# GpSimd's 512-column elementwise passes of a four-layer graph network, each made as two of 256 columns

## The chip, the cores and the metric

One core of one Trainium2 chip. The metric is the device time of the kernel in microseconds (us). The engines are TensorE (PE in the profile; PEld is its weight load), VectorE (DVE), ScalarE (ACT), GpSimd (POOL) and SyncE (SP).

## The reference, cut to what matters

128 graphs of 128 nodes with 256 features pass through four layers that share one adjacency matrix. Each layer takes `h = relu(layernorm(x))` and adds its result to `x`:

```python
h = relu(layernorm(x)); x = x + L0(h, adj)  # 4-head graph attention, elu, second attention, elu, ffn, layernorm
h = relu(layernorm(x)); x = x + L1(h, adj)  # 8-head attention: (softmax(q k^T) v) Wo^T + bo; its mask is adj == 0
h = relu(layernorm(x)); x = x + L2(h, adj)  # deg * (h Wi^T + b) + adj @ (h Wj^T)
h = relu(layernorm(x)); x = x + L3(h, adj)  # graph attention over 128 features, joined with them
```

Inside L0 the step `y = relu(out @ w1 + b1) @ w2 + b2 + out` is followed by a layernorm with `ln_gamma` and `ln_beta`.

## The kernel before, in words

The graphs are worked on in 64 pairs. The features of a pair lie in a slot of `xs` (128 partitions, 2 graphs of 256 columns; eight slots in rotation). Letters name stages: A and B are the heads of L0 and its first output, C is its second attention and ffn, D and F are L1, E is L2 and then L3.

Every engine runs the same loop, `rounds`: in round i it makes each step of its own list (`PE_ORDER`, `ACT_ORDER`, `DVE_ORDER`, `POOL_ORDER`) once, for pair i minus the number behind the step's name. So seven or more pairs are in work at a time, at different stages, and each engine's order is fixed by hand. A step waits at its head for semaphores of the steps before it (`done`, `both`, `before`) and counts up one of its own at its end.

Products are made from fp32 values split into a high part (rounded, type fp32r) and a low part (the rest), in three matmuls each. The split of a tile is an ACT copy to the high part and a subtraction for the low part.

GpSimd's list is `A_fleft A_fright A_rstd E_right E_rstd3 C_hb C_low B_lowh.1 D_xb E_fcopy E_rstd C_xb C_fcopy C_rstd E_xb D_rstd B_lowh.0`. Its steps are:

- `B_lowh` (line 464), once a graph: the low part of the upper 512 columns of `B_e`, for the matmuls `B_wh2` and `B_wh3` of PE (line 1191). The lower 512 columns are split by DVE (`B_lowl`, line 897).
- `C_low` (line 470): the low part of the ffn's hidden tile, 512 columns, for PE's `C_ffn` (line 1084, `pC<-w_high,C_hid_high`).
- `C_xb` (477), `D_xb` (487), `E_xb` (493): a bias row is added in place to the pair's slot, both graphs at once by `on_pair`, a broadcast. DVE's `C_x1` (945), `F_x2` (1002) and `E_mi` (1015) add to the slot later.
- `C_hb` (482): `C_h_t` plus `b2` into `C_hb_t`, for DVE's `C_y` (930).
- `E_fcopy` (lines 432 to 438): four small passes that split the two logit vectors of L3 in three bf16 parts. It waits for ACT's `E_hc` (699), and PE's `E_fT` (line 1200, `pE<-ident_bf,E_f`) waits for it.
- the `rstd` steps (413 and 415), which DVE's normalisations `A_z`, `D_z`, `E_z` and `E_z3` (all line 828) wait for, and others of up to 256 columns.

On DVE, `A_norm.0` and `A_norm.1` (line 881) scale the softmax of a graph, 512 columns, from SBUF to SBUF.

Of the kernel before, what the change touches and what calls it, by code (L numbers as in the profile page):

```python
# [4 lines left out]
ALU = mybir.AluOpType  # L5
ACT = mybir.ActivationFunctionType
AX = mybir.AxisListType
F32 = mybir.dt.float32
# [59 lines left out]
def gnn_stack(nc, x, adj, w_heads, a_heads, w_out, a_out, w1, b1, w2, b2, gamma, beta,  # L68
# [5 lines left out]
    K = D // P  # L74
    G = 2
    W = G * P
    H0 = w_heads.shape[0]
    HD = H0 * D
# [7 lines left out]
    with ExitStack() as ctx:  # L86
        def sb(name, shape, dt=F32):
            return ctx.enter_context(nc.sbuf_tensor(name, shape, dt))
# [4 lines left out]
        def sem(name):  # L93
            return ctx.enter_context(nc.semaphore(name))
# [19 lines left out]
        b2_b = sb("b2_b", [P, D])  # L114
        gamma_b = sb("gamma_b", [P, D])
        beta_b = sb("beta_b", [P, D])
# [3 lines left out]
        bo_b = sb("bo_b", [P, D])  # L120
        bl2_b = sb("bl2_b", [P, D])
        w3_w = sb("w3_w", [P, K, F3 + 2])

        def high_low(name, shape):
            return sb(name + "_high", shape, F32R), sb(name + "_low", shape, F32R)
# [30 lines left out]
        B_e = sb("B_e", [P, HD])  # L156
        B_hl_t = high_low("B_h", [P, HD])
# [5 lines left out]
        C_e, C_h_t = sb("C_e", [P, G, D]), sb("C_h_t", [P, G, D])  # L163
        C_hb_t = C_e
        C_hT_hl = high_low("C_hT", [P, K * W])
        C_hid_t = sb("C_hid_t", [P, K * W])
        C_hid_hl = high_low("C_hid", [P, K * W])
# [50 lines left out]
        S = {name: sem(name) for name in STEP_SEMAPHORES}  # L218
# [14 lines left out]
        def slot(g):  # L233
            return xs[:, (g // G) % PAIR_SLOTS, g % G, :]

        def pair_slot(p):
            return xs[:, p % PAIR_SLOTS, :, :]

        def done(eng, name, n):

            eng.wait_ge(S[name], n + 1)

        def both(eng, name, p):

            eng.wait_ge(S[name], G * p + G)
# [25 lines left out]
        def of_graph(make):  # L271

            return [lambda p, s=s: make(G * p + s, p, s) for s in range(G)]
# [7 lines left out]
        def on_pair(row):  # L281
            return row.unsqueeze(1).to_broadcast([P, G, D])
# [19 lines left out]
        def at_first(p, eng, signal, count):  # L302

            if p == 0:
                eng.wait_ge(signal, count)
# [49 lines left out]
        def _(pool):  # L355
# [104 lines left out]
            def B_lowh(g, p, s):  # L460

                done(pool, "B_highh", g)
                cols = slice(HD // 2, HD)
                pool.tensor_tensor(B_hl_t[1][:, cols], B_e[:, cols], B_hl_t[0][:, cols].bitcast(F32), ALU.subtract)\  # L464
                    .then_inc(S["B_lowh"], 1)

            def C_low(p):

                done(pool, "C_high", p)
                pool.tensor_tensor(C_hid_hl[1][:, :], C_hid_t[:, :], C_hid_hl[0][:, :].bitcast(F32), ALU.subtract)\  # L470
                    .then_inc(S["C_low"], 1)

            def C_xb(p):

                both(pool, "A_z", p)
                at_first(p, pool, weights_loaded, LOADED)
                pool.tensor_tensor(pair_slot(p), pair_slot(p), on_pair(beta_b[:, :]), ALU.add).then_inc(S["C_xb"], 1)

            def C_hb(p):

                both(pool, "C_h", p)
                pool.tensor_tensor(C_hb_t[:, :, :], C_h_t[:, :, :], on_pair(b2_b[:, :]), ALU.add).then_inc(S["C_hb"], 1)

            def D_xb(p):

                both(pool, "D_z", p)
                pool.tensor_tensor(pair_slot(p), pair_slot(p), on_pair(bo_b[:, :]), ALU.add).then_inc(S["D_xb"], 1)

            def E_xb(p):

                both(pool, "E_z", p)
                at_first(p, pool, dots_made, BIASES + 2)
                pool.tensor_tensor(pair_slot(p), pair_slot(p), on_pair(bl2_b[:, :]), ALU.add).then_inc(S["E_xb"], 1)

            def E_right(p):

# [3 lines left out]
                pool.tensor_tensor(right, right, E_h_t[:, :, 0:F3], ALU.add).then_inc(S["E_right"], 1)  # L500

            B_lowh = of_graph(B_lowh)
            rounds(pool, POOL_ORDER, {
                "A_rstd": rstd("A", "", A_mv, A_ve, A_rs), "C_rstd": rstd("C", "", C_mv, C_ve, C_rs),
# [3 lines left out]
                "C_fcopy": split_in_three("C", wh2[:, :, D:D + 2], C_f3, C_frest_t),  # L508
                "E_fcopy": split_in_three("E", E_h_t[:, :, F3:F3 + 2], E_f3, E_frest_t),
                "B_lowh.0": B_lowh[0], "B_lowh.1": B_lowh[1], "C_low": C_low,  # L510
                "C_xb": C_xb, "C_hb": C_hb, "D_xb": D_xb, "E_xb": E_xb, "E_right": E_right,
            }, {("A_fleft", 0): wh_low, ("B_lowh.0", 0): wout_low, ("C_hb", 0): other_low((W1, W2)),
                ("D_rstd", 0): other_low((WK, WV, WQ)), ("D_xb", 0): other_low((WO, WIJ))})
# [958 lines left out]
```

## Time and profile before

| | |
|---|---|
| runs | 2681.39, 2682.44, 2683.78 us; median 2682.44 |
| the profiled execution | 2683.62 us; its span, first to last instruction, 2681.8 us |
| PE, PEld busy | 2580.8 us (96%), 2333.0 us (87%) |
| DVE, ACT, POOL busy | 2304.7 (86%), 2061.2 (77%), 1248.4 us (47%) |
| granted TensorE clock, mean | 0.987 |
| DMA | 17 GB/s mean |

A busy share counts the time in which an engine has an instruction in work. PE's matmuls are pipelined, so one that is listed at 0.28 us can be followed by the next after 0.12 us. The idle time before an instruction, with what ended it, stands in square brackets in the timeline.

### The profile page before, as it was taken

What the parts mean: (1) busy time and instruction counts of PE and PEld (TensorE: products, weight loads), DVE (VectorE), ACT (ScalarE), POOL (GpSimd) and SP (SyncE); (2) the same over time, 40 slices, a digit from 0 to 9 for tenths busy, and PEclk for the clock granted to TensorE, in tenths of its full rate; (3) what the DMA queues carried; (4) which work ended last, traced back from release to release, by engine and by line L of the source; (5) the groups of instructions that cost most, each with busy time, mean ns of one, the idle gap of its engine ahead of it and who ended that gap; (6) DMA issues with size and microseconds to landing.
All of it is one profiled execution on the core that took longest, in us unless ns stands there. A gap on an engine that the chain in (4) does not pass through costs nothing.

```text
span 2681.8 us, 64380 instructions
## 1 busy us (share of the span) xinstructions
PE 2580.8 (96%) x21761; PEld 2333.0 (87%) x21761; DVE 2304.7 (86%) x8352; ACT 2061.2 (77%) x5708; POOL 1248.4 (47%) x2015
## 2 busy tenths in 40 slices
PE   4899999999999999999999999999999999999985
PEld 3789999998998998999999999899999899999874
DVE  5689889889888888888888888888988988988884
ACT  4688788787787887877877877878878878878752
POOL 3545445444444444454454454454544544544431
PEclk9999999999999999999999999999999999999986
DMA  4000000000000000000000000000000000000000
GB/s 131 1 2 9 17 17 9 17 17 14 13 17 13 13 17 17 10 17 17 10 17 17 10 17 17 10 17 17 9 17 17 9 17 17 10 17 13 9 9 12
DMA packets 41286, 44.29 MB, mean 17 GB/s; under 512 B 2816, under 2 KB 40448, under 8 KB 40832
## 3 DMA queue, kind: packets, MB, share of 16 engines
q1 hardware_dynamic: 40816, 39.14, 4.6%
q8 instruction: 175, 2.87, 0.5%
q14 instruction: 151, 1.24, 0.2%
q10 hardware_dynamic: 144, 1.05, 0.1%
HBM read 23.40 MB, written 16.78 MB: 15 GB/s over the span
## 4 chain that ended last, share of the span: by engine, by line
PE 70%; ACT 20%; POOL 4%; issue 3%; DVE 2%; SPq 1%; DMA 0%; ACTq 0%; DVEq 0%; POOLq 0%
PE pA L1084 12%; PE pB L1191 11%; PE pE L1084 7%; PE pB L1158 7%; PE pB L1084 7%; ACT probs L579 7%; PE pF L1315 4%; PE pC L1084 3%; ACT pA L573 3%; ACT B_h_high L613 2%; PE pF L1328 2%; PE pA L1302 2%; PE pC L1237 2%; ACT C_hid_t L649 2%; ACT whs L560 1%
## 5 line engine op out<-in xcount | busy, mean ns | idle before, releaser
L677 ACT ACTIVATE F_s_t<-F_s_t,F_m 128x128 f32<-128x128 f32 x1024 | 325.3, 395 | 0.9 <-DVE F_m L863 0.8
L1191 PE MATMUL pB<-wout_high,B_h_high 128*128 128x258 f32 x1024 | 307.4, 300 | 1.1 <-DVE B_h_low L897 1.1
L1191 PE MATMUL pB<-wout_low,B_h_high 128*128 128x258 f32 x1024 | 289.6, 283 | 0.0
L1191 PE MATMUL pB<-wout_high,B_h_low 128*128 128x258 f32 x1024 | 288.8, 282 | 0.0
L1158 PE MATMUL pB<-probs,whs 128*128 128x128 f32 x2048 | 285.4, 282 | 1.4 <-ACT wh L620 1.1
L1158 PEld LDWEIGHTS pB<-probs,whs 128*128 128x128 f32 x2048 | 254.2, 192 | 20.8 <-issue 2.4
L1084 PE MATMUL pA<-wh_high,A_hT_high 128*128 128x512 f32 x512 | 229.0, 447 | 9.5 <-POOL wh_low L388 8.4
L889 DVE SCALAR_TENSOR_TENSOR B_e<-B_e,pB 128x512 f32<-128x512 f32 x256 | 172.9, 675 | 71.7 <-ACT B_e L605 71.4
L464 POOL TENSOR_TENSOR B_h_low<-B_e,B_h_high 128x512 fp32r<-128x512 f32 x128 | 165.8, 1295 | 111.8 <-ACT B_h_high L613 111.8
L1084 PE MATMUL pA<-wh_high,A_hT_low 128*128 128x512 f32 x512 | 202.9, 396 | 0.0
L1084 PE MATMUL pA<-wh_low,A_hT_high 128*128 128x512 f32 x512 | 202.7, 396 | 0.0
L1191 PEld LDWEIGHTS pB<-wout_high,B_h_high 128*128 128x128 f32 x1024 | 193.9, 189 | 9.2 <-DVE B_h_low L897 1.9
L579 ACT ACTIVATE probs<-probs,A_m 128x128 f32<-128x128 f32 x512 | 198.2, 405 | 0.0
L1191 PEld LDWEIGHTS pB<-wout_low,B_h_high 128*128 128x128 f32 x1024 | 194.8, 190 | 2.7
L413 POOL TENSOR_TENSOR D_ve<-D_mv,eps 128x2 f32<-128x2 f32 x64 | 12.5, 195 | 395.2 <-DVE D_mv L821 395.2
L1191 PEld LDWEIGHTS pB<-wout_high,B_h_low 128*128 128x128 f32 x1024 | 193.8, 189 | 0.0
L470 POOL TENSOR_TENSOR C_hid_low<-C_hid_t,C_hid_high 128x512 fp32r<-128x512 f32 x64 | 83.2, 1300 | 236.1 <-ACT C_hid_high L546 236.1
L828 DVE TENSOR_SCALAR E_z_t<-xs,E_mv,E_rs 128x256 f32<-128x256 f32 x256 | 182.1, 731 | 3.2 <-POOL E_rs L415 3.2
L413 POOL TENSOR_TENSOR E_ve<-E_mv,eps 128x2 f32<-128x2 f32 x128 | 25.0, 195 | 333.8 <-DVE E_mv L821 333.8
L975 DVE TENSOR_REDUCE F_sum<-F_s_t 128x4 f32<-128x512 f32 x256 | 167.6, 676 | 0.2 <-ACT F_s_t L677 0.2
L613 ACT ACTIVATE B_h_high<-B_e 128x512 fp32r<-128x512 f32 x256 | 155.5, 640 | 7.6 <-DVE B_e L889 1.5
L605 ACT ACTIVATE B_e<-B_e 128x512 f32<-128x512 f32 x256 | 160.4, 627 | 0.1
(261 smaller groups left out, 10046.6 us busy)
## 6 DMA issues: line engine op xcount, KB each, us to landing
xs<-in_x SPq DMA_DIRECT2D x64, 256.0 KB, 2.7
out_x<-xs SPq DMA_DIRECT2D x64, 256.0 KB, 2.1
probs<-in_a_heads ACTq DMA_DIRECT2D x1, 1024.0 KB, 4.9
F_pT<-in_w_heads SPq DMA_DIRECT2D x2, 512.0 KB, 6.9
xs<-in_w_out SPq DMA_DIRECT2D x1, 1024.0 KB, 9.6
F_s_t<-in_wijT SPq DMA_DIRECT2D x1, 512.0 KB, 6.4
C_h_t<-in_a_out SPq DMA_DIRECT2D x1, 256.0 KB, 9.9
D_q_t<-in_w SPq DMA_DIRECT2D x1, 256.0 KB, 7.2
```

Of the source, the lines that this page charges most:

```text
L464: pool.tensor_tensor(B_hl_t[1][:, cols], B_e[:, cols], B_hl_t[0][:, cols].bitcast(F32), ALU.subtract)\
L579: last = act.activation(A_l[:, s, h, :], A_l[:, s, h, :], ACT.Exp, scale=-1.0, bias=A_m[:, s, h:h + 1], accum_out=A_sum[:, s, h:h + 1])
L605: act.activation(B_e[:, cols], B_e[:, cols], ACT.Exp, scale=-1.0).then_inc(S["B_exp" + part], 1)
L613: act.activation(B_hl_t[0][:, cols], B_e[:, cols], ACT.Copy).then_inc(S["B_high" + part], 1)
L677: last = act.activation(F_s_t[:, s, h, :], F_s_t[:, s, h, :], ACT.Exp, scale=-1.0, bias=F_m[:, s, h:h + 1])
L828: dve.tensor_scalar(z[:, s, :], slot(g), mv[:, s, 0:1], rs[:, s:s + 1], ALU.subtract, ALU.mult)\
L889: dve.scalar_tensor_tensor(out=e, in0=e, scalar=-1.0, in1=pB[:, bank, :], op0=ALU.add, op1=ALU.max)\
L975: dve.tensor_reduce(total, e, AX.X, ALU.add).then_inc(S["F_sum" + part], 1)
L1084: last = pe.matmul(dst, a, b, start=(i == 0), stop=(i == len(terms) - 1))
L1158: last = pe.matmul(pB[:, bank, (k % 4) * P:(k % 4 + 1) * P], whs[:, s, h, c * P:(c + 1) * P], attnT[:, s, h, :], start=True, stop=True)
L1191: last = pe.matmul(pB[:, 0, 0:D + 2], a, w[:, k, :], start=(k == 0 and i == 0), stop=(k == KH - 1 and i == 2))
L1315: last = pe.transpose(pF[:, c, j * P:(j + 1) * P], F_s_t[:, s, c * HPC + j, :], ident[:, :])
```

## The change

Each of the six steps makes its pass in two halves of 256 columns, one behind the other, with the semaphore counted up by the second. `B_lowh` runs twice a pair, so seven passes a pair become fourteen, and 448 passes in all become 896. The operands, the order of the steps, all waits and the other engines' programs stay as they are.

```diff
             def B_lowh(g, p, s):
 
                 done(pool, "B_highh", g)
-                cols = slice(HD // 2, HD)
-                pool.tensor_tensor(B_hl_t[1][:, cols], B_e[:, cols], B_hl_t[0][:, cols].bitcast(F32), ALU.subtract)\
-                    .then_inc(S["B_lowh"], 1)
+                for part in range(2):
+                    cols = slice(HD // 2 + part * HD // 4, HD // 2 + (part + 1) * HD // 4)
+                    last = pool.tensor_tensor(B_hl_t[1][:, cols], B_e[:, cols], B_hl_t[0][:, cols].bitcast(F32), ALU.subtract)
+                last.then_inc(S["B_lowh"], 1)
...
             def D_xb(p):
 
                 both(pool, "D_z", p)
-                pool.tensor_tensor(pair_slot(p), pair_slot(p), on_pair(bo_b[:, :]), ALU.add).then_inc(S["D_xb"], 1)
+                for s in range(G):
+                    last = pool.tensor_tensor(slot(G * p + s), slot(G * p + s), bo_b[:, :], ALU.add)
+                last.then_inc(S["D_xb"], 1)
...
```

`C_low` is cut in the same way as `B_lowh` (columns `c * W` to `(c + 1) * W` for c of 0 and 1), and `C_xb`, `C_hb` and `E_xb` in the same way as `D_xb`.

## Rows read from the trace of the kernel before

**Rows 1.** The page, part 1: busy time and share of each engine.

```profile
PE 2580.8 (96%) x21761; PEld 2333.0 (87%) x21761; DVE 2304.7 (86%) x8352; ACT 2061.2 (77%) x5708; POOL 1248.4 (47%) x2015
```

**Rows 2.** Busy time by stretch; columns PE, PEld, DVE, ACT, POOL busy, clock, DMA, GB/s.

```profile
1000.00:1500.00 500.00, 497.12 (x4257) 452.28 (x4256) 445.75 (x1636) 400.81 (x1125) 239.91 (x390) 1.00 0.05 14
```

**Rows 3.** The waits: who waited for whom, us in total, times, longest.

```profile
PE pE L1200 <- POOL E_f L438: 16.3, 61, 1.6
```

**Rows 4.** Timeline of PE in one round: start us, us, engine, line.

```profile
1324.57 0.60 PE L1151 MATMUL pA<-ident,probs 128*128 128x128 f32 x4
1325.40 0.22 PE L1200 MATMUL pE<-ident_bf,E_f 128*12 128x128 bf16 x1 [0.23 <-POOL E_f L438]
```

**Rows 5.** Timeline of POOL in the same round, and the same step a round on.

```profile
1312.92 1.28 POOL L482 TENSOR_TENSOR C_e<-C_h_t,b_b 128x512 f32<-128x512 f32 x1
...
1319.86 1.29 POOL L464 TENSOR_TENSOR B_h_low<-B_e,B_h_high 128x512 fp32r<-128x512 f32 x1 [0.74 <-ACT B_h_high L613]
1321.11 1.28 POOL L487 TENSOR_TENSOR xs<-xs,bo_b 128x512 f32<-128x512 f32 x1
1323.71 0.25 POOL L432 TENSOR_TENSOR E_f<-E_h_t,zeros 128x4 bf16<-128x4 f32 x1 [1.31 <-ACT E_h_t L699]
...
1324.32 0.63 POOL L436 TENSOR_TENSOR E_f<-E_frest_t,zeros 128x4 bf16<-128x4 f32 x1
1325.03 0.31 POOL L438 TENSOR_TENSOR E_f<-E_frest_t,E_f 128x4 bf16<-128x4 f32 x1
...
1326.46 1.27 POOL L477 TENSOR_TENSOR xs<-xs,beta_b 128x512 f32<-128x512 f32 x1
```

**Rows 6.** Timeline of DVE in the same round.

```profile
1313.49 1.20 DVE L828 TENSOR_SCALAR E_z_t<-xs,E_mv,E_rs 128x256 f32<-128x256 f32 x2
...
1321.90 0.69 DVE L930 TENSOR_TENSOR C_y_t<-pC,C_e 128x512 f32<-128x512 f32 x1
1322.51 0.40 DVE L828 TENSOR_SCALAR A_z_t<-xs,A_mv,A_rs 128x256 f32<-128x256 f32 x1
...
1324.21 0.68 DVE L881 TENSOR_TENSOR probs<-probs,A_rec 128x512 f32<-128x512 f32 x1
...
1326.53 1.35 DVE L828 TENSOR_SCALAR E_z_t<-xs,E_mv,E_rs 128x256 f32<-128x256 f32 x1
```

**Rows 7.** Timeline of ACT in the same round: what `E_fcopy` waits for.

```profile
1323.26 0.37 ACT L699 ACTIVATE E_h_t<-pE 128x260 f32<-128x260 f32 x1
```

**Rows 8.** Groups of POOL by line and shape: busy us, mean ns, idle before, releaser.

```profile
L487 POOL TENSOR_TENSOR xs<-xs,bo_b 128x512 f32<-128x512 f32 x64 | 82.8, 1294 | 0.0
L500 POOL TENSOR_TENSOR xs<-xs,E_h_t 128x256 f32<-128x256 f32 x64 | 43.8, 684 | 0.0
L413 POOL TENSOR_TENSOR D_ve<-D_mv,eps 128x2 f32<-128x2 f32 x64 | 12.5, 195 | 395.2 <-DVE D_mv L821 395.2
```

**Rows 9.** Who waited for line 464, and (second row) for line 470: us, times.

```profile
  PEld pB L1191: 0.2, 1
...
  PEld pC L1084: 0.2, 1
```

**Rows 10.** Groups of DVE by line and shape, columns as in rows 8.

```profile
L828 DVE TENSOR_SCALAR E_z_t<-xs,E_mv,E_rs 128x256 f32<-128x256 f32 x256 | 182.1, 731 | 3.2 <-POOL E_rs L415 3.2
L828 DVE TENSOR_SCALAR A_z_t<-xs,A_mv,A_rs 128x256 f32<-128x256 f32 x128 | 50.9, 398 | 1.2 <-POOL A_rs L415 1.2
```

**Rows 11.** The chain that ended last, in the drain: start us, us, what.

```profile
2567.33 1.11 DVE xs L945
...
2598.54 1.10 DVE xs L945
```

**Rows 12.** Timeline of POOL and DVE (last row: an undisturbed `C_x1`) beside that chain.

```profile
2566.89 1.26 POOL L493 TENSOR_TENSOR xs<-xs,bl_b 128x512 f32<-128x512 f32 x1 [1.09 <-DVE E_z_t L828]
...
2598.10 1.27 POOL L493 TENSOR_TENSOR xs<-xs,bl_b 128x512 f32<-128x512 f32 x1 [1.93 <-DVE E_z_t L828]
...
1336.56 0.48 DVE L945 SCALAR_TENSOR_TENSOR xs<-C_y_t,C_rs,xs 128x256 f32<-128x256 f32 x1
```

More of the change, by code:

```diff
@@ L462, in B_lowh @@
                 done(pool, "B_highh", g)
-                cols = slice(HD // 2, HD)
-                pool.tensor_tensor(B_hl_t[1][:, cols], B_e[:, cols], B_hl_t[0][:, cols].bitcast(F32), ALU.subtract)\
-                    .then_inc(S["B_lowh"], 1)
+                for part in range(2):
+                    cols = slice(HD // 2 + part * HD // 4, HD // 2 + (part + 1) * HD // 4)
+                    last = pool.tensor_tensor(B_hl_t[1][:, cols], B_e[:, cols], B_hl_t[0][:, cols].bitcast(F32), ALU.subtract)
+                last.then_inc(S["B_lowh"], 1)
             def C_low(p):
                 done(pool, "C_high", p)
-                pool.tensor_tensor(C_hid_hl[1][:, :], C_hid_t[:, :], C_hid_hl[0][:, :].bitcast(F32), ALU.subtract)\
-                    .then_inc(S["C_low"], 1)
+                for c in range(K):
+                    cols = slice(c * W, (c + 1) * W)
+                    last = pool.tensor_tensor(C_hid_hl[1][:, cols], C_hid_t[:, cols], C_hid_hl[0][:, cols].bitcast(F32),
+                                              ALU.subtract)
+                last.then_inc(S["C_low"], 1)
             def C_xb(p):
@@ L476, in C_xb @@
                 at_first(p, pool, weights_loaded, LOADED)
-                pool.tensor_tensor(pair_slot(p), pair_slot(p), on_pair(beta_b[:, :]), ALU.add).then_inc(S["C_xb"], 1)
+                for s in range(G):
+                    last = pool.tensor_tensor(slot(G * p + s), slot(G * p + s), beta_b[:, :], ALU.add)
+                last.then_inc(S["C_xb"], 1)
             def C_hb(p):
                 both(pool, "C_h", p)
-                pool.tensor_tensor(C_hb_t[:, :, :], C_h_t[:, :, :], on_pair(b2_b[:, :]), ALU.add).then_inc(S["C_hb"], 1)
+                for s in range(G):
+                    last = pool.tensor_tensor(C_hb_t[:, s, :], C_h_t[:, s, :], b2_b[:, :], ALU.add)
+                last.then_inc(S["C_hb"], 1)
             def D_xb(p):
                 both(pool, "D_z", p)
-                pool.tensor_tensor(pair_slot(p), pair_slot(p), on_pair(bo_b[:, :]), ALU.add).then_inc(S["D_xb"], 1)
+                for s in range(G):
+                    last = pool.tensor_tensor(slot(G * p + s), slot(G * p + s), bo_b[:, :], ALU.add)
+                last.then_inc(S["D_xb"], 1)
             def E_xb(p):
@@ L492, in E_xb @@
                 at_first(p, pool, dots_made, BIASES + 2)
-                pool.tensor_tensor(pair_slot(p), pair_slot(p), on_pair(bl2_b[:, :]), ALU.add).then_inc(S["E_xb"], 1)
+                for s in range(G):
+                    last = pool.tensor_tensor(slot(G * p + s), slot(G * p + s), bl2_b[:, :], ALU.add)
+                last.then_inc(S["E_xb"], 1)
             def E_right(p):
```

## Prediction

> **What bounds the kernel now.** I read the page's busy times first. PE is in work for 96% of the span, DVE for 86%, POOL, the only engine whose program changes, for 47% [rows 1]. The page's shares are averages, so next the view by stretch: in 500 us of the steady state PE is busy for 497.12 us at a granted clock of 1.00, POOL for 239.91 [rows 2]. So TensorE sets the pace there, and a change on POOL shows only where PE waits for POOL, directly or through DVE or ACT. The view of the waits has one such wait that repeats: `E_fT` on PE (line 1200) waits for the last small pass of `E_fcopy` on POOL, 61 times, 16.3 us in total [rows 3], 0.27 us a round. That is all that PE could get back from POOL in the steady state, and the place where it could lose.
>
> The timeline shows how this wait comes about. ACT ends `E_hc` at 1323.26 + 0.37 = 1323.63 [rows 7]. POOL has been idle for 1.31 us and starts the first of four small passes at 1323.71; the third takes 0.63 us, from 1324.32 to 1324.95, and the last ends at 1325.34 [rows 5]. PE stands ready behind its transposes and starts at 1325.40 [rows 4]. Beside the third pass DVE runs `A_norm.1`, 512 columns from SBUF to SBUF, from 1324.21 to 1324.89 [rows 6]: POOL starts 0.11 us behind it and is held until about its end. The reverse is seen as well. `E_z.0` takes 1.35 us on DVE where `C_xb` runs on POOL from 1326.46 to 1327.73 [rows 5, 6]; `A_z`, of the same operation and shape, has a mean of 0.398 us against 0.731 for the `E_z` group [rows 10]. So DVE and POOL hold each other up, and whoever starts second waits. From 1.35 - 0.40 = 0.95, DVE starts in effect at 1327.48, 0.25 us ahead of the recorded end of the pass: the pass lets go about 0.2 us before its record ends.
>
> The Trainium skill (SBUF — State Buffer, "Who interferes with whom") says that the two engines share a pair of ports which the first holds for its whole instruction while the other blocks. The trace agrees, but for those 0.2 us.
>
> **The change part by part.** All six edits have one cost and one possible gain, so they go together.
>
> *The cost.* 7 passes a pair by 64 pairs are 448 more instructions on POOL. No pass of this kernel is one of those halves; the nearest row is `E_right`, an addition of 256 columns, 684 ns, against 1294 ns for 512 [rows 8]. Two halves are 1368 ns, so a cut costs 0.074 us. It is bounded from above by the smallest pass, 195 ns for two columns [rows 8], which is all fixed cost, and from below by 0.04: records of neighbours overlap by 0.04 us (line 464 ends at 1321.15, line 487 starts at 1321.11 [rows 5]), so a second half hides that much of the 0.074. A gain isn't excluded by arithmetic but nothing in the rows suggests it. I take 0.074, as the nearest in shape. That is 448 x 0.074 = 33 us of POOL's busy time (18 to 87), and 1248 becomes about 1281 us, 48% of the span.
>
> The Trainium skill (Perfetto Trace Analysis, "GPSIMD Engine Instruction") warns that GpSimd's recorded durations are unreliable and wants start-to-start spacing. By it the cut would cost nearer 0.04 than 0.074, 18 us of POOL in place of 33; either lies under idle time.
>
> *What hides it.* Behind each pass I look at who waits for it and what is queued behind it. Line 464 was waited for once in 128 times, line 470 once in 64, for 0.2 us each [rows 9]; for the four bias passes nobody waited. POOL's queue has idle stretches that take up what a longer pass pushes on: `B_lowh.1` has 0.74 us ahead of it, and `D_xb` is followed by 1.31 us [rows 5]. The tightest place is this last one: `B_lowh.1` and `D_xb` are together 2 x 0.074 = 0.15 us longer, `D_xb` ends at 1322.54 instead of 1322.39, and `E_fcopy` still starts at 1323.71, released by ACT. So PE's wait gets neither longer nor shorter by the queue. Cost on the path: 0.
>
> *What DVE gains.* Between two halves POOL lets go for some 0.2 us, and I expect DVE to get in. `E_z.0` at 1326.53 would then wait until about 1326.9 in place of 1327.5, 0.6 us less. For `E_z3` (two in a row from 1313.49, beside `C_hb`, [rows 5, 6]) the first starts earlier, but the second half of `C_hb` can come between the two, so their sum may stay. In the steady state DVE spends it all as idle time: `A_norm.1` follows `C_y`, and `C_y` at 1321.90 follows the end of a PE product. DVE being early elsewhere doesn't move these two. So `A_norm.1` still starts 0.11 us before POOL's third small pass, and the wait of 0.27 us a round stays. Gain in the steady state: 0.
>
> *The drain.* In the last 115 us PE is not always what the chain runs through. The chain holds `C_x1` twice at 1.11 and 1.10 us [rows 11], where an undisturbed one takes 0.48 [rows 12]; each time `E_xb` (line 493) had started on POOL 0.4 us before. With halves, the first lets go at about 2567.35 and 2598.55, as `C_x1` comes up: 0.6 us saved, twice. Cuts that lie on the chain cost at most a few times 0.074. Sum: -1.2 us, with 0 (the next wait takes it) and -3 (the `E_z3` places gain too) as its bounds.
>
> The profiled execution took 2683.62 us, 1.2 above the median of 2682.44; the sum makes it 2682.4, and the median 2681.2. A measurement can tell about 0.2% (5.4 us) from no change, so I forecast none.
>
> **The rivals.**
>
> *DVE's freed time reaches PE* (faster). DVE loses 256 x (0.731 - 0.398) = 85 us in the `E_z` group alone [rows 10], and halves take over half of it away. If that moved `A_norm.1` or `E_hc` relative to one another, so that the small passes run free, PE's whole wait would go: -16.3 us, and 2666; half of it -8, 2674. For it speaks the length of those waits. Against it: `C_y` is tied to PE and the rest of DVE's row to `C_y`. Chance 8%. The Trainium skill (SBUF — State Buffer, "Summary: rules for kernel authors") advises to schedule whichever of the two engines is off the critical path; read by itself, a shorter hold can only help.
>
> *`D_xb`'s second half meets `A_z.0`* (slower). `A_z.0` starts at 1322.51 and `D_xb` lets go at about 1322.39 - 0.22 = 1322.17 [rows 5, 6]. If both cuts together cost over 0.34 us, 0.17 each (the upper bound is 0.195), `A_z.0` is held, all behind it on DVE slips, and `A_norm.1` holds POOL's third small pass longer. That grows to 0.11 us a round, since a later `A_norm.1` comes behind the small pass and lets it go first. 61 x 0.11 = +6.7 us: 2689. For it: the margin is small and the price is from another step. Against: the price would have to be double. Chance 7%.
>
> *The lock isn't let go between halves* (the change does nothing for DVE). Then DVE's waits stay, the drain gains nothing, and each place there costs 0.07: 2682.4 + 0.3 = 2682.7. Chance 10%, inside no change.
>
> **How the numbers follow.** The forecast, 2681.2, has 75%, its own range 2678 to 2684 from the drain's bounds and the spread of the runs. With the third case no change has 85%, faster 8%, slower 7%. The range takes in both of those and goes half way to the others, as partial shifts of the wait are possible: 2676 to 2687.
>
> **What would show it.** Right: POOL busy up by 18 to 87 us with halves near 0.68 us; the `E_z` group's mean down from 0.731 towards 0.55; the PE wait for line 438 still about 16 us, 61 times. Wrong: that wait gone, or grown past 20 us; `A_z.0` longer than 0.45 us; a new PE wait for line 464's or 470's successor.

## The result, and the profile after

The changed kernel takes 2687.45 us (median of 20 runs, 2684.06 to 2689.65) against 2682.50 us (20 runs, 2678.66 to 2684.56): a ratio of 1.0019, interval 1.0012 to 1.0026. It is slower by 5 us, just under the 0.2% that I had called no change, and 0.45 us above the end of my range. The profiled execution took 2685.24 us, a span of 2683.4 us.

First the lines of the page that answer to [rows 1], and the stretch of [rows 2], of the kernel after:

```profile
PE 2583.1 (96%) x21761; PEld 2330.2 (87%) x21761; DVE 2278.0 (85%) x8352; ACT 2061.2 (77%) x5708; POOL 1320.8 (49%) x2463
```

```profile
1000.00:1500.00 500.00, 497.06 (x4250) 451.11 (x4249) 439.24 (x1626) 399.79 (x1120) 254.63 (x478) 1.00 0.05 14
```

POOL is busy for 72 us more, DVE for 27 us less, and PE's busy time hardly moves. Busy shares don't show the loss. Neither does the one wait that I had watched; in the waits after, it is 16.5 us, where [rows 3] had 16.3:

```profile
PE pE L1212 <- POOL E_f L438: 16.5, 61, 1.6
```

What shows it is the length of a round. PE's `E_fT` of the third and of the 58th pair, in the timeline of PE, before (first two rows) and after:

```profile
286.64 0.22 PE L1200 MATMUL pE<-ident_bf,E_f 128*12 128x128 bf16 x1 [0.22 <-POOL E_f L438]
...
2484.30 0.22 PE L1200 MATMUL pE<-ident_bf,E_f 128*12 128x128 bf16 x1 [0.22 <-POOL E_f L438]
```

```profile
286.29 0.22 PE L1212 MATMUL pE<-ident_bf,E_f 128*12 128x128 bf16 x1 [0.23 <-POOL E_f L438]
...
2489.04 0.22 PE L1212 MATMUL pE<-ident_bf,E_f 128*12 128x128 bf16 x1 [0.23 <-POOL E_f L438]
```

That is 2197.66 / 55 = 39.957 us a round before and 2202.75 / 55 = 40.050 after: 0.093 us each, 5.1 us over these 55. From the second mark to the end the kernel before takes 2681.8 - 2484.3 = 197.5 us, the one after 194.4, and the fill is 0.35 us shorter, so the two profiled executions differ by 1.6 us only. But not all of these 3.5 us can be put down to the change. The two executions had different granted clocks of TensorE, 0.987 and 0.989 in the mean. Part of the difference lies at their ends, as the last 35 us of both show (columns as in [rows 2], before and then after):

```profile
2646.80:2681.80 35.00, 16.20 (x50) 10.22 (x47) 8.23 (x29) 5.61 (x17) 4.33 (x10) 0.50 0.04 15
```

```profile
2648.40:2683.40 35.00, 14.91 (x52) 9.57 (x52) 8.70 (x33) 5.61 (x17) 5.93 (x16) 0.63 0.04 15
```

The changed kernel by itself took 2688.9 us in its two runs with a mean clock of 0.987 and 2686.0 in the ten with 0.989, 2.8 us apart, so most of the 3.5 goes with the clock. The medians of 20 runs differ by 4.95 us, about what the rounds alone lose.

Comparing the starts of PE's matmuls within a round, before and after, one place stands out: the first matmul of `A_wh_lo.0`, about 9.8 us behind `E_fT`. The timeline of PE there, before and then after:

```profile
1334.94 0.40 PE L1084 MATMUL pA<-wh_high,A_hT_low 128*128 128x512 f32 x1
1335.17 0.49 PE L1084 MATMUL pA<-wh_high,A_hT_high 128*128 128x512 f32 x1
```

```profile
1337.09 0.40 PE L1096 MATMUL pA<-wh_high,A_hT_low 128*128 128x512 f32 x1
1337.45 0.50 PE L1096 MATMUL pA<-wh_high,A_hT_high 128*128 128x512 f32 x1
```

From start to start it is 0.23 us before and 0.36 after. This is no accident of one round: counted from `E_fT`, and in the median of 51 rounds, the starts of PE's groups of matmuls up to here agree within 0.01 us, and this one is 0.13 us later. PE isn't listed as idle, since each record lasts 0.40 us, longer than the gap. The step waits for `A_frest` (DVE, line 858 before and 870 after). DVE before, then DVE and POOL after:

```profile
1332.89 0.70 DVE L945 SCALAR_TENSOR_TENSOR xs<-C_y_t,C_rs,xs 128x256 f32<-128x256 f32 x1
1334.68 0.43 DVE L858 TENSOR_TENSOR A_f_t<-pA,A_f_t 64x256 fp32r<-64x256 f32 x1
```

```profile
1335.04 0.84 DVE L957 SCALAR_TENSOR_TENSOR xs<-C_y_t,C_rs,xs 128x256 f32<-128x256 f32 x1
1336.97 0.43 DVE L870 TENSOR_TENSOR A_f_t<-pA,A_f_t 64x256 fp32r<-64x256 f32 x1
```

```profile
1334.19 1.41 POOL L504 TENSOR_TENSOR xs<-xs,bl_b 128x256 f32<-128x256 f32 x2 [1.39 <-DVE E_z_t L840]
```

`E_xb` takes 1.41 us in halves where it took 1.26 and 1.27 whole [rows 12]. Its second half had begun at 1334.87, before `C_x1.0` came up at 1335.04; so `C_x1.0` is held to the end of both halves as it was by the whole pass, and that end is 0.14 us later. From the end of `C_x1.0` to the start of `A_frest` DVE has other work and no idle time, 1.09 us in both kernels, so `A_frest` is later by as much. It ended at 1335.11 before, 0.06 us ahead of the matmul: it had no slack. In the view of PEld's waits the same is a line of its own, which was there before and has grown:

```profile
PEld pA L1084 <- DVE A_f_t L858: 15.6, 58, 0.3
```

```profile
PEld pA L1096 <- DVE A_f_t L870: 23.5, 58, 0.4
```

### The profile page after: what moved, and what is told of

Same layout as the page of the kernel before. It is cut to its first block, busy times and chain, and to the rows that moved or that the text cites. A ratio compares the mean times of both kernels' runs of the same rounds, so it can differ in the third digit from the quotient of the medians.

```text
span 2683.4 us, 64828 instructions
## 1 busy us (share of the span) xinstructions
PE 2583.1 (96%) x21761; PEld 2330.2 (87%) x21761; DVE 2278.0 (85%) x8352; ACT 2061.2 (77%) x5708; POOL 1320.8 (49%) x2463
## 3 DMA queue, kind: packets, MB, share of 16 engines
q14 instruction: 155, 1.27, 0.2%
## 4 chain that ended last, share of the span: by engine, by line
PE 71%; ACT 20%; POOL 4%; issue 3%; DVE 2%; SPq 1%; DMA 0%; ACTq 0%; DVEq 0%; POOLq 0%
PE pA L1096 12%; PE pB L1203 11%; PE pB L1170 7%; PE pE L1096 7%; PE pB L1096 7%; ACT probs L591 7%; PE pF L1327 4%; PE pC L1096 3%; ACT pA L585 3%; ACT B_h_high L625 2%; PE pF L1340 2%; PE pA L1314 2%; PE pC L1249 2%; ACT C_hid_t L661 2%; ACT whs L572 1%
## 5 line engine op out<-in xcount | busy, mean ns | idle before, releaser
L465 POOL TENSOR_TENSOR B_h_low<-B_e,B_h_high 128x256 fp32r<-128x256 f32 x256 | 183.7, 739 | 103.0 <-ACT B_h_high L625 103.0
L473 POOL TENSOR_TENSOR C_hid_low<-C_hid_t,C_hid_high 128x256 fp32r<-128x256 f32 x128 | 92.3, 743 | 218.4 <-ACT C_hid_high L558 218.4
L610 ACT ACTIVATE B_e<-pB 128x512 f32<-128x512 f32 x256 | 152.9, 597 | 5.9 <-PE pB L1170 5.8
```

What stands on the lines that cost most here:

```text
L465: last = pool.tensor_tensor(B_hl_t[1][:, cols], B_e[:, cols], B_hl_t[0][:, cols].bitcast(F32), ALU.subtract)
L610: act.activation(B_e[:, cols], pB[:, bank, :], ACT.Relu, scale=-1.0).then_inc(S["B_neg" + part], 1)
```

## The experiments

Theory A: the loss comes through `E_xb` alone, by `C_x1.0`, `A_frest` and PE's `A_wh_lo.0`. Theory B: it is spread over all 448 cuts, as the price of more instructions on POOL. Every ratio is to the kernel before on the same chip: 2681.51 us for the first four experiments, 2681.15 for the next four and 2681.78 for the last.

**`E_xb` whole again.**

```diff
-                for s in range(G):
-                    last = pool.tensor_tensor(slot(G * p + s), slot(G * p + s), bl2_b[:, :], ALU.add)
-                last.then_inc(S["E_xb"], 1)
+                pool.tensor_tensor(pair_slot(p), pair_slot(p), on_pair(bl2_b[:, :]), ALU.add).then_inc(S["E_xb"], 1)
```

> The change with only E_xb made whole again (64 of the 448 cuts undone). Theory A (the loss comes through E_xb: its two halves end 0.14 us later than the whole pass, the C_x1 that DVE starts beside it is held 0.14 us longer, A_frest behind it is 0.14 us later, and PE's A_wh_lo.0 starts late by as much): the loss goes, rounds back to 39.96 us, C_x1.0 back to 0.71 us from 0.85, time 2680 to 2683 against 2682.5 before. Theory B (the loss is the number of POOL instructions or is spread over all cuts): six sevenths of it stay, 2686 to 2687.

Measured 2676.74 us, ratio 0.9981 (0.9973 to 0.9990). Theory B falls. But the time is better than A had it, below the kernel before, and so is the round: 39.89 us. The other cuts gain something in each round.

**Only `E_xb` cut,** the same edit the other way round, on the kernel before.

> The kernel before with only E_xb cut in two. Theory A: the whole loss of the steady state, 0.09 to 0.10 us a round, 2687 to 2689 (the other cuts' savings in the drain are missing). Theory B: one seventh of the loss, 2683.

Measured 2688.88 us, ratio 1.0028 (1.0019 to 1.0037), a round of 40.08 us. That is as theory A had it. One seventh of the cuts costs more than all of them together.

**All cuts, `E_xb` later.**

```diff
                 both(pool, "E_z", p)
                 at_first(p, pool, dots_made, BIASES + 2)
+                if p + 2 < PAIRS:
+                    done(pool, "C_x1", G * (p + 2))
```

> The change with all cuts kept, and one wait added: E_xb of a pair starts only after the C_x1.0 that it ran beside. Theory A: C_x1.0 is held by nothing, 0.48 us, A_frest 0.36 us earlier than in the change, PE's A_wh_lo.0 no longer waits, 2680 to 2683. If the number or length of POOL's passes counts by itself: stays at 2687.

Measured 2671.73 us, ratio 0.9967 (0.9954 to 0.9979), a round of 39.81 us: the time is 8 us below the expected range. PEld's waits for `A_frest` are gone:

```profile
PEld pA L1098 <- DVE A_f_t L872: 0.4, 2, 0.2
```

The expectation left out that a whole `E_xb` costs something at this place too: against the version with `E_xb` whole, at 39.89, it is 0.075 us a round. The run also excludes another reading, that the steps behind `E_xb` in POOL's queue are what came too late: here both halves start 1.5 us later than in the change, and the loss is gone.

**`E_xb` cut as 384 + 128 columns.**

```diff
-                for s in range(G):
-                    last = pool.tensor_tensor(slot(G * p + s), slot(G * p + s), bl2_b[:, :], ALU.add)
+                for cols in (slice(0, 192), slice(192, D)):
+                    x = xs[:, p % PAIR_SLOTS, :, cols]
+                    last = pool.tensor_tensor(x, x, bl2_b[:, cols].unsqueeze(1).to_broadcast([P, G, cols.stop - cols.start]),
+                                              ALU.add)
                 last.then_inc(S["E_xb"], 1)
```

> The change with E_xb cut as 384 + 128 columns in place of 256 + 256, so as many passes and as many columns. The first pass should start its successor about 0.98 us after its own start, at about 7.6 us after the round's mark, and C_x1.0 comes up at 7.49, between the two. Theory A with DVE let in between two passes: C_x1.0 takes about 0.5 us instead of 0.85, A_frest early, 2680 to 2683. If the lock is not let go between two passes, or if the sum of passes counts: C_x1.0 stays at 0.8 us or more, 2687.

Measured 2674.32 us, ratio 0.9973 (0.9963 to 0.9983), 6 us below the expected range, for the same reason. The trace comes from one more execution of the same kernel:

> The change with E_xb cut as 384 + 128 columns, once more for its profile: C_x1.0 about 0.5 us, started between the two passes, rounds 39.81 to 39.89 us.

That one took 2671.95 us, a round of 39.82 us. The timeline of DVE and of POOL in it:

```profile
1329.36 0.47 DVE L959 SCALAR_TENSOR_TENSOR xs<-C_y_t,C_rs,xs 128x256 f32<-128x256 f32 x1
```

```profile
1328.51 1.64 POOL L505 TENSOR_TENSOR xs<-xs,bl_b 128x384 f32<-128x384 f32 x2 [1.39 <-DVE E_z_t L842]
```

`C_x1.0` starts inside the 1.64 us of the two passes, 0.10 us before the second (1329.46), and isn't held at all. So DVE does get in between two passes. As many passes and as many columns as in the change, one boundary moved, and the kernel is 12 us faster (0.9973 of the kernel before against 1.0019). What counts is where a boundary lies when DVE comes up.

**The gain of the other cuts.** Theory A was extended: `E_z3` runs beside `C_hb`, and if the pair ends earlier, so does `D_vc` behind it (line 952), on which PE's `B_oh.1` waits. Theory C: the gain comes from another cut.

Only `C_hb` cut, on the kernel before:

```diff
-                pool.tensor_tensor(C_hb_t[:, :, :], C_h_t[:, :, :], on_pair(b2_b[:, :]), ALU.add).then_inc(S["C_hb"], 1)
+                for s in range(G):
+                    last = pool.tensor_tensor(C_hb_t[:, s, :], C_h_t[:, s, :], b2_b[:, :], ALU.add)
+                last.then_inc(S["C_hb"], 1)
```

> The kernel before with only C_hb cut in two. Theory A (the gain of the other cuts, 0.07 us a round, comes through E_z3 and D_vc, on which PE's B_oh.1 waits): 39.89 us a round, 2676 to 2679. Theory C (it comes from C_xb's or B_lowh's cuts): 2682.

Measured 2679.31 us, ratio 0.9994 (0.9985 to 1.0002): by the times alone not clear of none. The round of its profile is 39.89 us, as with all cuts but `E_xb`, and in the median of 51 rounds PE's start of `B_ol.1` and `B_oh.1` (line 1158 before) is 0.05 us earlier.

`B_lowh`, `C_low`, `C_xb` and `D_xb` cut, the two others whole (the edits are those of the change):

> The kernel before with B_lowh, C_low, C_xb and D_xb cut, C_hb and E_xb whole: 320 of the 448 cuts. Theory A: 39.96 us a round, 2680 to 2683, no change; a cut beside which no one waits costs and gains nothing. Theory C: 2677. Theory B (each cut costs something): 2685.

Measured 2680.78 us, ratio 0.9997 (0.9988 to 1.0006), a round of 39.93 us. These 320 cuts move nothing that the times can tell. The round is 0.03 us shorter all the same, though neither `A_wh_lo.0` nor `B_oh.1` starts earlier in it, so a difference of that size between two traces stays unexplained.

**Whole passes, two of them later.** If only the meetings count, no cuts are needed:

```diff
                 both(pool, "C_h", p)
+                if p >= 3:
+                    both(pool, "E_z3", p - 3)
...
                 at_first(p, pool, dots_made, BIASES + 2)
+                if p + 2 < PAIRS:
+                    done(pool, "C_x1", G * (p + 2))
```

> The kernel before, whole passes, with two added waits: E_xb behind the C_x1.0 it ran beside, and C_hb behind the E_z3 pair it ran beside. Theory A (only where a pass meets a DVE operation matters, cuts or no cuts): C_x1.0 0.48 us, E_z3 pair 0.75 us, D_vc 0.4 us earlier; A_wh_lo.0 and B_oh.1 on PE start without waiting; rounds 39.80 or less, 2668 to 2673, as good as the version with cuts and a late E_xb. If the cuts gain something by themselves: 2676 or more.

Measured 2667.43 us, ratio 0.9950 (0.9937 to 0.9962), a round of 39.71 us, a little better than expected. DVE's `E_z3` pair and `D_vc` behind it, in its timeline:

```profile
1345.11 0.73 DVE L832 TENSOR_SCALAR E_z_t<-xs,E_mv,E_rs 128x256 f32<-128x256 f32 x2
1345.76 0.68 DVE L956 TENSOR_TENSOR D_v_t<-pB,bv_b 128x512 f32<-128x512 f32 x1
```

and PE beside them:

```profile
1346.57 0.60 PE L1079 MATMUL pE<-ident,E_z_t 128*128 128x128 f32 x4
1347.00 1.06 PE L1162 MATMUL pB<-probs,whs 128*128 128x128 f32 x8
```

The pair took 1.20 us in the kernel before [rows 6]. The matmuls of `B_ol.1` and `B_oh.1` (line 1162) now start 0.43 us behind the transposes, and the next matmul starts 0.81 us behind them, at 1347.81. In the kernel before it was 0.49 us and then 0.89, to 1356.23, as these two rows of its PE timeline have it:

```profile
1354.85 0.60 PE L1075 MATMUL pE<-ident,E_z_t 128*128 128x128 f32 x4
1355.34 1.13 PE L1158 MATMUL pB<-probs,whs 128*128 128x128 f32 x8
```

**`A_norm.1` later.** The wait of 0.27 us a round that [rows 3] show was the other thing to test. DVE's order in the kernel before becomes:

```diff
-C_stats.0:3 A_norm.0:1 A_recip.1:1 E_stats.1:5 A_norm.1:1 C_moments.0:3 A_z.1:0 E_moments.0:5 E_moments.1:5 E_fTc:6
-C_stats.1:3 C_g.0:3 E_z.0:5 C_moments.1:3 E_max.0:6 E_max.1:6 C_g.1:3 A_low:0 F_maxa.0:4 F_maxa.1:4 C_fTc:2 E_recip:6
+C_stats.0:3 A_norm.0:1 A_recip.1:1 E_stats.1:5 C_moments.0:3 E_moments.0:5 E_moments.1:5 C_stats.1:3 A_norm.1:1 A_z.1:0 E_fTc:6
+ C_g.0:3 E_z.0:5 C_moments.1:3 E_max.0:6 E_max.1:6 C_g.1:3 A_low:0 F_maxa.0:4 F_maxa.1:4 C_fTc:2 E_recip:6
```

> The kernel before, whole passes, with DVE's A_norm.1 and A_z.1 moved behind C_moments.0, E_moments.0, E_moments.1 and C_stats.1, some 0.6 us later. If E_fcopy's third small pass is late because A_norm.1 holds it: POOL's line 436 falls from 0.63 to 0.2 us, PE's wait for line 438 (0.27 us a round) goes, 0.2 to 0.27 us less a round, 2667 to 2671. If ACT's E_hc sets that wait, or A_norm.1 being later makes PE or ACT wait elsewhere: no change, 2682.

Measured 2663.94 us, ratio 0.9933 (0.9920 to 0.9945), a round of 39.64 us, somewhat better than expected.

**The two together,** whole passes with the two waits and the new order of DVE:

> The kernel before, whole passes, with the two added waits (E_xb behind C_x1.0, C_hb behind E_z3) and A_norm.1 and A_z.1 moved later on DVE. If the three are separate waits of PE, their gains add: 0.15 for the two waits and 0.2 to 0.27 for the move, a round of 39.5 to 39.6 us, 2655 to 2662. If PE's next wait takes their place: as the better of the two alone.

Measured 2648.96 us, ratio 0.9878 (0.9861 to 0.9894) against 2681.78: 33 us faster than before, and by the ratios 38 faster than the change. The round is 39.42 us, so the gains add nearly in full (0.25 and 0.32 us a round apart, 0.54 together), and both were larger than expected. Its POOL, DVE and PE at `E_fT`:

```profile
1309.11 0.20 POOL L436 TENSOR_TENSOR E_f<-E_frest_t,zeros 128x4 bf16<-128x4 f32 x1
1309.39 0.20 POOL L438 TENSOR_TENSOR E_f<-E_frest_t,E_f 128x4 bf16<-128x4 f32 x1
```

```profile
1309.44 0.69 DVE L885 TENSOR_TENSOR probs<-probs,A_rec 128x512 f32<-128x512 f32 x1
```

```profile
1309.79 0.22 PE L1204 MATMUL pE<-ident_bf,E_f 128*12 128x128 bf16 x1
```

The third small pass takes 0.20 us where it took 0.63 [rows 5]; `A_norm.1` starts behind both, and PE's row has no idle time in brackets any more. PE's wait for `E_fcopy` is 3.7 us in all in place of 16.3:

```profile
PE pE L1204 <- POOL E_f L438: 3.7, 4, 1.6
```

## Why the prediction was wrong

**The step that failed, in short.** The working put the steady state at nothing on both sides, "Cost on the path: 0" and "Gain in the steady state: 0". Measured, the steady state loses 0.093 us a round, 5.1 us over 55 rounds: +0.13 us where the halved `E_xb` holds DVE's `C_x1.0` longer and PE's `A_wh_lo.0` starts late by it, less some gain elsewhere in the round. Of the signs that were to tell right from wrong, those of being right came true (POOL busy by 72 us more, with halves of 0.73 us rather than 0.68, the `E_z` group's mean down to 0.596, the wait for line 438 at 16.5 us in 61 times) and of the others none but a single wait of 0.2 us for the successor of line 470: they watched other places. And 0.2% was too coarse a limit for no change, since with 20 runs a side the interval of the ratio is 0.14% wide.

**What bounds the kernel: right, but read too coarsely.** TensorE sets the pace, and POOL matters only where PE waits for it. The failing sentence is "That is all that PE could get back from POOL in the steady state, and the place where it could lose." It came from the list of PE's own waits, in which a wait shorter than the record of the matmul ahead of it doesn't appear. There were two more such places in each round, both on DVE's results: `A_frest`, which PEld's list had with 15.6 us in 58 times, and `D_vc`, which no list had. Taking away three meetings gave 33 us, where I had 16.3 as the most. The wait that I had named gave 17 of them by itself; the two other meetings gave 14 by themselves.

**The price of a cut: half of what was measured.** I had 0.074 us (0.04 to 0.195) from `E_right`. The groups of POOL by line and shape, after, have the halves of `E_xb`

```profile
L504 POOL TENSOR_TENSOR xs<-xs,bl_b 128x256 f32<-128x256 f32 x128 | 91.0, 732 | 91.4 <-DVE E_z_t L840 91.4
```

at 732 ns, and two of them take 1.41 us: the cut costs 0.14 to 0.15 us, twice my value and within its bounds. My lower bound has a slip: 0.074 less the hidden 0.04 is 0.034, not 0.04. All 448 cuts added 72 us of busy time, 0.16 each, of which I had forecast 33, with 87 as the end; it is more than 0.15 because DVE holds some halves in turn (`C_hb`'s have a mean of 0.80 us).

**What hides it: right for six of the seven passes a pair, wrong for one.** The 320 cuts of the last experiment on parts cost nothing measurable, and `C_hb` gained a little. For `E_xb` I wrote that "for the four bias passes nobody waited". No one waited for its semaphore. But DVE was held by the pass itself, and no semaphore carries that wait, it only makes the record longer: `C_x1.0` took 0.70 us in place of 0.48, and `A_frest` behind `C_x1.0` was what PE needed. In the drain I had seen that very meeting and priced it as a gain; in the steady state I didn't look at it. Measured, it is +0.09 us a round for the whole change and +0.12 for `E_xb` alone.

**What DVE gains: half right.** `E_z.0` fell from 1.35 to 0.81 us, near the 0.6 I had, and it did turn into idle time: behind the next operation DVE now stands idle for 0.49 us. So the third rival, that the lock isn't let go between halves, is out. `E_z3` kept nearly its sum, as said, since the second half came between the two. What failed is "In the steady state DVE spends it all as idle time": the 0.04 us that the pair did gain went through `D_vc` to PE. That `D_vc` carries it is read from the code and the starts; no run changed `D_vc` alone, and none moved the whole `C_hb` alone.

**The drain: right in place, its size not shown.** I had -1.2 us, at most -3. The profiles have about -3 from the 58th `E_fT` to the end, but most of that goes with the clock of the two executions, as said with the result. The medians leave little for the fill and the drain together, and a round read from one trace is too coarse to say how much. What the trace does show is one hold that got shorter. The chain after holds `C_x1` there with

```profile
2570.90 0.57 DVE xs L957
```

in place of the 1.11 us of [rows 11]; the second one is no longer on it.

**The rivals.** The slower one had the right kind of mechanism, a second half that ends too late for DVE, at the wrong place: I named `D_xb` and `A_z.0`, which didn't meet, and not `E_xb` and `C_x1.0`, which did. Its threshold of 0.17 us a cut came from the slack of that place; at `E_xb` the slack was nothing, so any price decided. `A_z.0` takes 0.40 us before and after.

**What stays open.** The parts don't add up exactly: `E_xb` alone costs 0.12 us a round on the kernel before, but 0.16 on the version with all other cuts (from 39.89 to 40.05). Both have the same 0.13 us at `A_wh_lo.0`; where the rest goes wasn't tried. In the medians of PE's starts the kernel before loses some 0.05 us a round along `C_ffn` and the matmuls behind it that most of the others don't lose, cut or whole, and no one start stands out there.

## What to carry to other kernels

Cutting a pass on GpSimd doesn't make it yield to VectorE by itself: it moves the moments at which VectorE can get in, and it makes the pass longer. So find every meeting of the two engines in a round, ask what TensorE takes from the VectorE work behind it, and move one of the two by a wait or an order; here two waits and one new order gave 33 us where the cuts lost 5. And read the bound engine's slack from the starts of its matmuls and from the waits of its weight loads, since short waits vanished under the pipelined records here.

## What the runs showed of the hardware

- DVE gets in between two passes of POOL that stand one behind the other, if it comes up before the second has begun: `C_x1.0` took 0.47 us inside the 384 + 128 columns, and 0.84 where it came 0.17 us after the second half's start.
- An addition on POOL takes 0.73 us for 256 columns in `E_xb` and 1.28 for 512. Two halves one behind the other overlap a little and take 1.41, so some 0.14 us more.
- The hold works both ways: a pass of 4 columns on POOL takes 0.20 us free and 0.63 behind a 512-column operation of DVE, and `C_x1.0`, 256 columns on DVE, takes 0.48 us free and 0.70 behind the whole `E_xb` of POOL.
- Executions of one kernel took longer where TensorE was granted less clock: the changed kernel's ten runs at a mean of 0.989 have a median of 2686.0 us, its two at 0.987 one of 2688.9. In the profiles before and after, the last 35 us had 0.50 and 0.63.
